# A decoder block for 16 sequences on one core: the second FFN layer as three reduced-precision products

## The chip, the cores and the metric

The program runs on one core of a Trainium2 chip, in one launch. The metric is the device time in microseconds (us). The kernel before was timed three times: 994.58, 998.78 and 999.22 us, median 998.78.

The core's engines work in parallel, each through its own list of instructions in order: PE (TensorE, matrix products into the eight PSUM banks), DVE (VectorE), ACT (ScalarE), POOL (GpSimd), and SP (SyncE), which here only issues DMA transfers. They wait for each other through semaphores.

## The reference, cut to what matters

For each of 16 sequences `x[b]` of 256 tokens by 256 dimensions, with 16 heads of 16 dimensions:

```
x = layernorm(x + self_attention(x))        # q, k: rms norm and rope; causal softmax
x = layernorm(x + cross_attention(x, ctx))  # causal and key mask
x = layernorm(x + ffn(x))

ffn(x) = gelu(rms(x, gamma_l) @ w1_l.T + b1_l) @ w2_l.T + b2_l     # hidden 128, "light"
       + heavy path on the 256 tokens of highest score               # hidden 1024
```

Top-k picks 256 of 256 tokens, and the scores end as factors of one, so the heavy path is applied to every token. The kernel therefore stacks both paths into one FFN with 9 hidden chunks of 128 (`FCH = 9`).

## The kernel before

The weights stay in SBUF. The work of the 16 sequences is a software pipeline written out by hand: `iterations` unrolls steps i = -2 to 19. Step i does the self attention of sequence s = i, most of the cross attention of c = i-1, the end of the cross attention of f = i-2, and the FFN of l = i-3. So an FFN runs in steps 3 to 18, and in steps 3 to 15 all stages are live.

A step has four phases on PE, each a loop over the 16 heads:

- **S1**: `scores(1, s, h)`, the self-attention scores. Each head is three products: the causal mask (`cmaskb`, through the identity), and two blocks of q times k. DVE takes the row maxima from the bank (`mx`, L899). Between heads PE does `hidden(l, j)`, the first FFN layer, at the places of `HIDDEN_AT`.
- **S2**: `scores(2, c, h)`, the same for cross attention. Between heads: transposes of q and k of the next sequence, the value projection, and `ffn_out(l, 0, j)`, the second FFN layer for the first 128 tokens.
- **T1**: `scores_t(1, s, h)`, transposed scores; ACT takes the exponential (`pr`, L746), POOL zeroes the masked part (L1217), and PE multiplies by the values. Between heads `ffn_out(l, 1, j)` for the other 128 tokens.
- **T2**: the same for cross attention, with the projections of later sequences.

Score banks are a ring of three: a head's scores wait until the bank of three heads earlier was read. Between S1 and S2, DVE runs `max_parts(1, s)`: six small operations, each waiting for the one before (L912 to L925), which turn the maxima into three bf16 parts. DVE does the first maximum of S2 only after them.

fp32 products are either plain (`w,g` in `ffn_out`: two PE instructions each) or three products of high and low parts in the type fp32r (`hidden`, and the q, k, v projections of L355 to L361: one PE instruction each). In `ffn_out` one product has 128 hidden rows, 128 tokens and 256 output columns, and there are 9 x 2 x 16 = 288 of them.

q and k are split into three bf16 parts (`nat`), which SP copies by DMA into stacks (`stk`) of 96 rows, six blocks of 16 rows, so that one product gives all cross terms. That is `stack_parts` (L288): 6 transfers of 128 KB for each of q and k.

POOL's list in a step: rope of the next sequence (`rotate`, L241: 12 operations on 128x256 or half of it), x plus bias for the FFN's residual (`x2b`, L1234), low halves of later inputs (`xTlow`, `ctxlow`), a copy, a root, then the masking. ACT's list in a step: copies, the nine gelus (`g`, L758), the table for the exponential, copies, the exponentials.

In the first steps DVE rotates sequence 0 itself, then cuts `wk2` and `wv2` in halves (`halve_cross`) and fills constant rows of the second stacks (`more_rows`), before the first maximum. Scaling and cutting `w1` (`scale_w1`, L1036) follows in step 0, all on DVE.

Of the kernel before, what the change touches and what calls it, by code (L numbers as in the profile page):

```python
# [43 lines left out]
P = 128  # L44
# [19 lines left out]
def build(nc, io):  # L64
# [4 lines left out]
    with ctx:  # L69
# [15 lines left out]
        w1h = sb("w1h", [P, C, FCH * P], f32r); w1l = sb("w1l", [P, C, FCH * P], f32r); w2 = sb("w2", [P, FCH, D])  # L85
# [6 lines left out]
        cmask = sb("cmask", [P, 2, P])  # L92
# [26 lines left out]
        mx2 = sb("mx2", [P, TT, H])  # L119
# [9 lines left out]
        g = sb("g", [P, FCH, T])  # L129
# [7 lines left out]

        w1raw = g[:, :, :].rearrange("p j t -> p (j t)").rearrange("p (c n) -> p c n", c=C)
# [21 lines left out]
        s_const = sem("consts_ready"); s_mask = sem("keybias_step"); s_rows = sem("fixed_rows_ready")  # L160
# [4 lines left out]
        s_qn = sem("qn_ready"); s_rot = sem("pool_rot"); s_rope = sem("rope_ready")  # L165
# [18 lines left out]
        s_h = sem("hidden_ready"); s_g = sem("gelu_ready"); s_out = sem("out_stored"); s_warm = sem("exp_table_loaded")  # L184
# [56 lines left out]
        def rotate(eng, ops, b):  # L241

            for t in range(TT):
# [6 lines left out]
                for s in range(2):  # L250
                    ops.tensor_tensor(qc[:, t, s * D:(s + 1) * D].rearrange("p (h d) -> p h d", d=HD),  # L251
                                    qn[:, t, s * D:(s + 1) * D].rearrange("p (h d) -> p h d", d=HD),
                                    ropeC[:, t, s:s + 1, :].to_broadcast([P, H, HD]), ALU.mult)
                    for half in range(2):
                        last = ops.tensor_tensor(rv[:, s, :, half, :], qv[:, s, :, 1 - half, :],  # L255
                                               ropeS[:, t, s:s + 1, half * h2:(half + 1) * h2]
                                               .to_broadcast([P, H, h2]), ALU.mult)
                last.then_inc(s_rot, 1)
                eng.wait_ge(s_rot, n + 1)

                for s in range(2):
# [3 lines left out]
                                           rot[:, t, s * D:(s + 1) * D].rearrange(pairs, c=C, d=HD), ALU.add)  # L265
                last.then_inc(s_rope, 1)
# [5 lines left out]
        def _(sp):  # L272
# [15 lines left out]
            def stack_parts(a, b, nth, s):  # L288

                terms = (TERMS_Q, TERMS_K)[s]  # L290
                for part, ready in ((0, s_hi[a]), (1, s_mid[a]), (2, s_split[a])):
                    sp.wait_ge(ready, 2 * b + nth + 1)
                    for r in range(len(terms)):
                        if terms[r] == part:
                            load(stk[a][s][r * HD:(r + 1) * HD, :, :], nat[a][s][:, part, :], s_stk[a])

            def stacks(a, b):

                wait(sp, s_st[a], H * b)
                if a == 2:  # L300
                    if first(b):
                        sp.wait_ge(s_rows, 5)
# [42 lines left out]
        def _(pe):  # L345
# [9 lines left out]
            def halves_proj(out, src, t, w):  # L355

                products = [(x, y, c) for x, y in ((src[0], w[0]), (src[0], w[1]), (src[1], w[0])) for c in range(C)]
                for n, (x, y, c) in enumerate(products):
                    last = mm(out, x[:, c, t * P:(t + 1) * P], y[:, c, :], n == 0, n == len(products) - 1)
# [16 lines left out]
            def qk1(b, t):  # L376

                pe.wait_ge(s_xlow, b + 1)
# [5 lines left out]
                halves_proj(bank[QK1_BANK[t]][:, :], xTp, t, wqk1).then_inc(s_qk1, 1)  # L384
# [53 lines left out]
            def hidden(b, j):  # L438

                if j == 0:  # L440
                    if first(b):
                        pe.wait_ge(s_w1, 1)
# [19 lines left out]
            def transpose_qk1(b):  # L462
                pe.wait_ge(s_rope, TT * (b + 1))
# [5 lines left out]

                if live(b - 2):  # L470
# [4 lines left out]
            def scores(a, b, h):  # L475

                if h == 0:
                    if first(b):
                        pe.wait_ge(s_rows, (None, 3, 5)[a])
# [4 lines left out]
                on_pe = a in MASKED_ON_PE  # L484
                if on_pe:
                    blocks = out[:, 0:3 * P].rearrange("p (k t) -> p k t", k=3)
                    mm(blocks[:, 0:3:2, :], idb[:, :], cmaskb[:, :, :], True, False, True)
                mm(out[:, 0:P], q[0:K_MAX, h, 0:P], kk[0:K_MAX, h, 0:P], not on_pe, not on_pe, True)
                mm(out[:, P:3 * P], q[0:K_MAX, h, P:T], kk[0:K_MAX, h, :], not on_pe, True, True)\
# [184 lines left out]
            pe.wait_ge(s_whalf, 2)  # L674
# [5 lines left out]
        def _(act):  # L680
# [53 lines left out]
            def exponential(a, b, h):  # L734
# [9 lines left out]
                else:  # L744
                    act.wait_ge(s_pv[2], NG * (b - 1) + 3 + h // HG)
                nc.scalar.activation(pr[:, h % (2 * HG), :], ring_bank("T", a, b, h)[:, 0:3 * P], ACT.Exp, scale=HD ** -0.5)\  # L746
                    .then_inc(s_exp[a], 1)

            def gelu(b, j):
                act.wait_ge(s_h, FCH * b + j + 1)  # L750
                if j == 0:
                    if first(b):
                        act.wait_ge(s_wffn, 16 * N_FFN)

                        act.wait_ge(s_w1, 1)
# [3 lines left out]
                    .then_inc(s_g, 1)  # L759

            def load_ffn():
                load(w1raw[:, :, 0:LIGHT * P], io["w1h"].rearrange(chunks, p=P), s_wffn)
                load(w1raw[:, :, LIGHT * P:FCH * P], io["w1l"].rearrange(chunks, p=P), s_wffn)
                load(w2[:, 0:LIGHT, :], io["w2h"].rearrange(chunks, p=P), s_wffn)
                load(w2[:, LIGHT, :], io["w2l"], s_wffn)
# [5 lines left out]
            def step(i):  # L771
# [55 lines left out]
                if first(i + 1):  # L827

                    act.wait_ge(s_stk[1], 16 * NSTK[1])
                    load_ffn()  # L830

# [27 lines left out]
        def _(dve):  # L859
# [30 lines left out]
            cm = cmask[:, :, :].rearrange("p k t -> p (k t)")  # L890

# [467 lines left out]
```

## Time and profile before

| | us |
|---|---|
| median of 3 runs | 998.78 |
| lowest, highest | 994.58, 999.22 |
| span of the profiled execution, first to last instruction | 995.1 |
| PE, DVE, ACT, POOL busy | 907.2, 735.8, 496.2, 486.2 |
| one step in the middle | 55.03 |

The profile gives the span of its execution and no separate time for it. The span is 3.7 us under the median, and 0.5 us over the lowest time. Busy time of PE is not PE at its peak, since the products overlap and their ends are modelled; the starts of consecutive instructions are what tell its pace.

### The profile page before, as it was taken

The numbers are of one execution on the slowest core, as the hardware profiler recorded it, in microseconds if no ns is written. First come the engines' busy times: TensorE is split into PE (matmuls) and PEld (weight loads), VectorE is DVE, ScalarE is ACT, GpSimd is POOL, SyncE is SP. The second block draws the span as 40 slices with busy tenths as digits, with TensorE's granted clock in tenths as the row PEclk, the third lists the DMA queues.
The fourth block names the chain that finished last, engine by engine and source line by source line (L and its number), as shares of the span: only waits on it lengthen the run. The fifth ranks groups of instructions, "written<-read, shape, count | busy, mean of one in ns | idle before, by whom it ended". The sixth has DMA issues, their size and how long they took to land.

```text
span 995.1 us, 21915 instructions
## 1 busy us (share of the span) xinstructions
PE 907.2 (91%) x7904; PEld 709.5 (71%) x7904; DVE 735.8 (74%) x1847; ACT 496.2 (50%) x1063; POOL 486.2 (49%) x899
## 2 busy tenths in 40 slices
PE   2467888999999999999999999999999999898896
PEld 2345565787878787787878787877878786777575
DVE  8777678677878878877778788888778787574612
ACT  1131443647465555646474655556464755455243
POOL 2173464545555564645464655646455546143221
PEclk9669899999999999999999999999999999999999
DMA  3909192836657290927566481909365563705000
GB/s 108 180 23 142 24 130 31 118 44 91 83 63 110 37 135 11 132 36 110 63 87 88 55 118 29 129 20 127 46 105 70 77 87 47 115 3 67 22 1 22
DMA packets 79644, 74.24 MB, mean 75 GB/s; under 512 B 8592, under 2 KB 78896, under 8 KB 79536
## 3 DMA queue, kind: packets, MB, share of 16 engines
q1 hardware_dynamic: 75872, 68.90, 49.9%
q10 hardware_dynamic: 3664, 3.94, 1.2%
q8 instruction: 63, 1.03, 0.5%
q14 instruction: 45, 0.37, 0.2%
HBM read 17.49 MB, written 4.20 MB: 22 GB/s over the span
## 4 chain that ended last, share of the span: by engine, by line
PE 56%; DVE 19%; issue 8%; POOL 5%; DMA 4%; SPq 3%; ACT 2%; POOLq 0%; ACTq 0%; DVEq 0%
PE bank L347 53%; DVE mx L899 8%; SPq L274 3%; POOL pr L1217 2%; DMA stk1k<-nat1k 2%; PE bank L372 2%; DVE x L980 2%; PE bank L571 2%; ACT pr L746 2%; DVE qn L1032 1%; DMA stk2q<-nat2q 1%; POOL rstd L1207 1%; DVE nat2q L882 1%; DVE nat2q L884 1%; DVE rest L875 1%
## 5 line engine op out<-in xcount | busy, mean ns | idle before, releaser
L746 ACT ACTIVATE pr<-bank 128x384 f32<-128x384 f32 x512 | 241.0, 501 | 192.4 <-PE bank L347 192.1
L899 DVE TENSOR_REDUCE mx<-bank 128x3 f32<-128x384 f32 x512 | 264.5, 551 | 82.5 <-PE bank L347 80.8
L1217 POOL TENSOR_SCALAR_AFFINE_SELECT pr<-pr 128x256 f32<-128x256 f32 x512 | 225.9, 453 | 183.1 <-ACT pr L746 179.9
L347 PE MATMUL bank<-cmaskb,idb 128*128 128x256 bf16 x512 | 145.2, 284 | 31.5 <-DVE mx L899 15.7
L347 PE MATMUL bank<-w,g 128*128 128x256 f32 x576 | 170.8, 389 | 1.1 <-ACT g L758 1.1
L758 ACT ACTIVATE g<-bank,b 128x256 f32<-128x256 f32 x144 | 68.4, 475 | 90.1 <-PE bank L347 89.8
L1241 POOL TENSOR_TENSOR xTlow<-xT,xThigh 128x512 fp32r<-128x512 f32 x16 | 21.2, 1324 | 161.1 <-ACT xThigh L682 161.1
L347 PEld LDWEIGHTS bank<-w,g 128*128 128x128 f32 x576 | 89.6, 190 | 5.2 <-ACT g L758 1.5
L347 PEld LDWEIGHTS bank<-cmaskb,idb 128*128 128x128 bf16 x512 | 50.3, 98 | 58.9 <-DVE mx L899 32.1
L347 PE MATMUL bank<-stk1k,stk1q 97*128 97x128 bf16 (+1 forms) x512 | 86.6, 258 | 0.0
L347 PE MATMUL bank<-stk1q,stk1k 100*128 100x256 bf16 (+1 forms) x512 | 80.0, 254 | 4.5 <-DMA stk1q<-mT 3.2
L347 PE MATMUL bank<-stk2k,stk2q 97*128 97x128 bf16 (+1 forms) x512 | 82.4, 247 | 0.0
L347 PE MATMUL bank<-stk2q,stk2k 100*128 100x256 bf16 (+1 forms) x512 | 73.0, 252 | 1.8 <-DMA stk2q<-mT 0.9
L347 PEld LDWEIGHTS bank<-stk1q,stk1k 100*128 100x128 bf16 x512 | 42.3, 99 | 38.4 <-ACT pr L746 8.6
L251 POOL TENSOR_TENSOR qc<-qn,ropeC 128x256 f32<-128x256 f32 x60 | 44.2, 737 | 46.6 <-DVE qn L1032 29.6
L347 PE MATMUL bank<-xnh,w1h 128*128 128x256 f32 x288 | 64.7, 306 | 2.3 <-DVE y L952 2.1
L347 PE MATMUL bank<-wo,onT 128*128 128x256 f32 x256 | 63.1, 390 | 1.9 <-ACT onT L682 1.9
L347 PEld LDWEIGHTS bank<-stk2k,stk2q 97*128 97x128 bf16 x512 | 50.6, 99 | 18.9
L255 POOL TENSOR_TENSOR sq<-qn,ropeS 128x128 f32<-128x128 f32 x120 | 60.7, 527 | 0.0
L347 PEld LDWEIGHTS bank<-stk1k,stk1q 97*128 97x128 bf16 x512 | 53.0, 103 | 10.1 <-issue 0.2
L347 PE MATMUL bank<-pr,va 128*32 128x256 f32 (+1 forms) x1024 | 57.1, 342 | 2.4 <-POOL pr L1217 2.3
L347 PE MATMUL bank<-xnl,w1h 128*128 128x256 f32 x288 | 57.6, 281 | 0.0
(157 smaller groups left out, 1829.3 us busy)
## 6 DMA issues: line engine op xcount, KB each, us to landing
stk1q<-nat1q SPq DMA_DIRECT2D x96, 128.0 KB, 4.6
stk1k<-nat1k SPq DMA_DIRECT2D x96, 128.0 KB, 6.5
stk2k<-nat2k SPq DMA_DIRECT2D x96, 128.0 KB, 4.7
stk2q<-nat2q SPq DMA_DIRECT2D x96, 128.0 KB, 6.1
xT<-in_xT SPq DMA_DIRECT2D x16, 256.0 KB, 7.2
ctxT<-in_ctxT SPq DMA_DIRECT2D x16, 256.0 KB, 7.8
x<-in_x SPq DMA_DIRECT2D x16, 256.0 KB, 6.1
out_x<-x SPq DMA_DIRECT2D x16, 256.0 KB, 5.9
```

The costliest lines, as they stand in the source:

```text
L251: ops.tensor_tensor(qc[:, t, s * D:(s + 1) * D].rearrange("p (h d) -> p h d", d=HD), qn[:, t, s * D:(s + 1) * D].rearrange("p (h d) -> p h ...
L255: last = ops.tensor_tensor(rv[:, s, :, half, :], qv[:, s, :, 1 - half, :], ropeS[:, t, s:s + 1, half * h2:(half + 1) * h2] .to_broadcast([ ...
L274: sp.dma_start(dst, src).then_inc(s, 16)
L347: return nc.tensor.matmul(out, lhsT, rhs, start=start, stop=stop, skip_group_check=check)
L372: last = nc.tensor.transpose(bank[k][:, c * T + t * P:c * T + (t + 1) * P], src[:, t, c * P:(c + 1) * P], idf[:, :])
L571: last = nc.tensor.transpose(bank[TOK_BANK[a][t]][:, gr * P:(gr + 1) * P], oT[:, gr, t * P:(t + 1) * P], idf[:, :])
L746: nc.scalar.activation(pr[:, h % (2 * HG), :], ring_bank("T", a, b, h)[:, 0:3 * P], ACT.Exp, scale=HD ** -0.5)\
L758: nc.scalar.activation(g[:, j, :], bank[HIDDEN_BANK[j % 2]][:, 0:T], ACT.Gelu, bias=b1[:, j:j + 1])\
L899: V.tensor_reduce(mx3[:, h, :], scored[:, 0:3 * P].rearrange("p (k t) -> p k t", k=3), AX.X, ALU.max, negate=True).then_inc(s_mx[a], 1)
L980: V.tensor_scalar(xo[a][:, t, :], y[a][:, t, :], mv[a][:, t, 0:1], rstd[a][:, t:t + 1], ALU.subtract, ALU.mult).then_inc(s_x[a], 1)
L1217: G.affine_select(out=slot, in_=slot, compare_op=ALU.is_ge, fill=0.0, base=0, pattern=[[0, 2], [1, P]], channel_multiplier=-1).then_inc(s_ ...
L1241: G.tensor_tensor(xTp[1][:, :, :], xT[:, :, :], xTp[0][:, :, :].bitcast(f32), ALU.subtract)\
```

## The change

- **FFN's second layer.** ACT copies each gelu result `g` to a high part `gh` (fp32r), POOL subtracts to a low part `gl`, and PE does `gh*w2h + gh*w2l + gl*w2h` in place of `g*w2`. `w2` is now loaded in step 0 into `g` and cut in step 1 (ACT `high_w2`, DVE the low half).
- **In place.** The layer norms write over their input (`xo = y`), so `add_residual` now waits for what `layer_norm` waited for. Rope multiplies `qn` in place (`qc = qn`): the sine products come first, with one more wait.
- **Stacks.** Row r of a 16-row part now goes to stack row 6r + n instead of 16n + r. Number and size of the transfers are the same.
- **First steps.** `rotate_first` rotates q of both halves before k, and PE transposes q at once. PE's first projection waits for its parts one by one. The constant rows of the second stacks are filled by POOL (`cross_rows`). `halve_cross` moves on DVE behind the self-attention maxima of step 0. `w1` is scaled and rounded on ACT (`high_w1`), and DVE does only the low half (`low_w1`).
- Code that nothing used is gone (`cmask`, `mx2`), and the SBUF set aside for DMA descriptors is cut to 1024.

```diff
-        xo = [None, sb("x1", [P, TT, D]), sb("x2", [P, TT, D]), sb("x3", [P, TT, D])]
+        xo = y
...
-        qn = sb("qn", [P, TT, 2 * D]); rot = sq; qc = sb("qc", [P, TT, 2 * D]); qr = sb("qr", [P, TT, 2 * D])
+        qn = sb("qn", [P, TT, 2 * D]); rot = sq; qc = qn; qr = sb("qr", [P, TT, 2 * D])
...
-                            load(stk[a][s][r * HD:(r + 1) * HD, :, :], nat[a][s][:, part, :], s_stk[a])
+                            load(stk[a][s][r:NPROD:len(terms), :, :], nat[a][s][:, part, :], s_stk[a])
...
                 if t == 0 and j == 0:
+                    if first(b):
+                        pe.wait_ge(s_w2, 1)
                     pe.wait_ge(s_g, FCH * (b + 1))
-                last = mm(bank[FFN_BANK][:, t * D:(t + 1) * D], g[:, j, t * P:(t + 1) * P], w2[:, j, :],
-                          j == 0, j == FCH - 1)
+                if t == 0:
+                    pe.wait_ge(s_gl, FCH * b + j + 1)
+                for n, (x, w) in enumerate(((gh, w2h), (gh, w2l), (gl, w2h))):
+                    last = mm(bank[FFN_BANK][:, t * D:(t + 1) * D], x[:, j, t * P:(t + 1) * P], w[:, j, :],
+                              j == 0 and n == 0, j == FCH - 1 and n == 2)
...
-                    wait(act, s_o[3], b)
+                    wait(act, s_gl, FCH * b)
...
+            def gelu_high(b, j):
+                act.wait_ge(s_g, FCH * b + j + 1)
+                if j == 0:
+                    wait(act, s_o[3], b)
+                copy(gh[:, j, :], g[:, j, :]).then_inc(s_gh, 1)
...
                     if live(l):
                         gelu(l, j)
+                        if j > 0:
+                            gelu_high(l, j - 1)
+                if live(l):
+                    gelu_high(l, FCH - 1)
...
+                if first(i):
+                    high_w1()
+                if first(i - 1):
+                    high_w2()
...
@@ def add_residual
-                wait(dve, s_x[a], TT * b)
+                if a == 1:
+                    wait(dve, s_x1t, b)
+                    wait(dve, s_x1c, b)
+                elif a == 2:
+                    wait(dve, s_x2b, b)
+                    wait(dve, s_xn, TT * b)
+                else:
+                    wait(dve, s_out, 16 * b)
...
@@ step of DVE
+                if first(i):
+                    halve_cross()
+                    scale_gammas()
...
                 if first(i):
-                    scale_w1()
+                    low_w1()
+                if first(i - 1):
+
+                    dve.wait_ge(s_w2h, 1)
+                    V.tensor_tensor(w2l[:, :, :], w2raw[:, :, :], w2h[:, :, :].bitcast(f32), ALU.subtract).then_inc(s_w2, 1)
...
-                if first(i + 1):
-                    halve_cross()
-                    more_rows()
...
@@ step of POOL, behind x2b
+                    for j in range(FCH):
+                        pool.wait_ge(s_gh, FCH * l + j + 1)
+                        G.tensor_tensor(gl[:, j, :], g[:, j, :], gh[:, j, :].bitcast(f32), ALU.subtract).then_inc(s_gl, 1)
```

The order of the instructions at two places. PE, from the end of S2 into T1 (`w,g` is the plain second layer). Before:

```order
L347 MATMUL bank<-stk2k,stk2q 128x256
L347 MATMUL bank<-w,g 128x256
L347 MATMUL bank<-stk1q,stk1k 128x256
L347 MATMUL bank<-stk1q,stk1k 128x128
L347 MATMUL bank<-w,g 128x256
L347 MATMUL bank<-stk1q,stk1k 128x256
```

And now:

```order
L378 MATMUL bank<-stk2k,stk2q 128x256
L378 MATMUL bank<-w2h,gh 128x256
L378 MATMUL bank<-w2l,gh 128x256
L378 MATMUL bank<-w2h,gl 128x256
L378 MATMUL bank<-stk1q,stk1k 128x256
L378 MATMUL bank<-stk1q,stk1k 128x128
L378 MATMUL bank<-w2h,gh 128x256
```

Each product became three, at the same place between the same heads.

POOL, from the rope of the next sequence to the masking. Before:

```order
L263 TENSOR_TENSOR qr<-qc,sq 128x8x32 x2
L1234 TENSOR_TENSOR x2b<-x,b2sum 128x512
L1241 TENSOR_TENSOR xTlow<-xT,xThigh 128x512
L1247 TENSOR_TENSOR ctxlow<-ctxT,ctxhigh 128x512
L1253 COPY x1c<-x 128x512
```

And now:

```order
L265 TENSOR_TENSOR qr<-qn,sq 128x8x32 x2
L1298 TENSOR_TENSOR x2b<-y,b2sum 128x512
L1303 TENSOR_TENSOR gl<-g,gh 128x256 x9
L1308 TENSOR_TENSOR xTlow<-xT,xThigh 128x512
L1316 TENSOR_TENSOR ctxlow<-ctxT,ctxhigh 128x512
L1322 COPY x1c<-y 128x512
```

Nine subtractions stand where POOL before went straight to `xTlow`.

## Rows read from the trace of the kernel before

**Rows 1.** The page: busy time of the engines.
```profile
PE 907.2 (91%) x7904; PEld 709.5 (71%) x7904; DVE 735.8 (74%) x1847; ACT 496.2 (50%) x1063; POOL 486.2 (49%) x899
```
**Rows 2.** Chain of work that ended last, two middle steps (start us, us, what).
```profile
487.22 11.62 PE bank L347 x84
...
542.25 11.62 PE bank L347 x84
```
**Rows 3.** Timeline of PE (start us, us, what, [idle before <-releaser]): S2, then T1.
```profile
542.25 0.28 PE L347 MATMUL bank<-cmaskb,idb 128*128 128x256 bf16 x1 [0.18 <-DVE mx L899]
...
548.95 0.27 PE L347 MATMUL bank<-cmaskb,idb 128*128 128x256 bf16 x1
...
549.65 0.27 PE L347 MATMUL bank<-cmaskb,idb 128*128 128x256 bf16 x1
...
549.93 0.27 PE L347 MATMUL bank<-cmaskb,idb 128*128 128x256 bf16 x1
...
551.75 0.65 PE L347 MATMUL bank<-w,g 128*128 128x256 f32 x2
552.23 0.33 PE L347 MATMUL bank<-stk1q,stk1k 100*128 100x256 bf16 x2
552.40 0.65 PE L347 MATMUL bank<-w,g 128*128 128x256 f32 x2
```
**Rows 4.** Timeline of PE: before and after twelve fp32r products in T2, six in S1.
```profile
506.09 0.33 PE L347 MATMUL bank<-stk2q,stk2k 100*128 100x256 bf16 x2
...
507.75 0.51 PE L347 MATMUL bank<-stk2q,stk2k 100*128 100x256 bf16 x4
...
538.27 0.27 PE L347 MATMUL bank<-cmaskb,idb 128*128 128x256 bf16 x1
...
539.26 0.28 PE L347 MATMUL bank<-cmaskb,idb 128*128 128x256 bf16 x1
```
**Rows 5.** Timeline of DVE: between S1 and S2, and in S2.
```profile
539.52 0.17 DVE L912 COPY nm<-mx 128x16 f32<-128x16 f32 x1
...
540.58 0.55 DVE L899 TENSOR_REDUCE mx<-bank 128x3 f32<-128x384 f32 x1
...
549.42 0.56 DVE L899 TENSOR_REDUCE mx<-bank 128x3 f32<-128x384 f32 x1 [0.15 <-PE bank L347]
```
**Rows 6.** Timelines of POOL and ACT in the same step.
```profile
534.30 1.26 POOL L1234 TENSOR_TENSOR x2b<-x,b2sum 128x512 f32<-128x512 f32 x1
546.06 1.27 POOL L1241 TENSOR_TENSOR xTlow<-xT,xThigh 128x512 fp32r<-128x512 f32 x1 [10.50 <-ACT xThigh L682]
...
539.46 0.47 ACT L758 ACTIVATE g<-bank,b 128x256 f32<-128x256 f32 x1 [0.81 <-PE bank L347]
```
**Rows 7.** Timelines of DVE and POOL in step 0, when both are at work.
```profile
55.96 0.60 DVE L919 CAST mp<-nm 128x32 bf16<-128x32 f32 x1
...
59.32 1.63 DVE L884 TENSOR_TENSOR nat1q<-rest,nat1q 128x512 bf16<-128x512 f32 x1
...
55.08 1.45 POOL L263 TENSOR_TENSOR qr<-qc,sq 128x256 f32<-128x256 f32 x2
58.96 1.44 POOL L1241 TENSOR_TENSOR xTlow<-xT,xThigh 128x512 fp32r<-128x512 f32 x1 [2.43 <-ACT xThigh L682]
```
**Rows 8.** Timelines of the first steps: DVE, then ACT.
```profile
44.37 1.76 DVE L1153 MEMSET stk2q<- 1x2048 f32 x1 [0.38 <-issue]
46.17 0.56 DVE L899 TENSOR_REDUCE mx<-bank 128x3 f32<-128x384 f32 x1
...
67.55 2.64 DVE L1050 TENSOR_TENSOR w1l<-g,w1h 128x2304 fp32r<-128x2304 f32 x1
...
61.65 0.49 ACT L746 ACTIVATE pr<-bank 128x384 f32<-128x384 f32 x1 [2.25 <-PE bank L347]
```
**Rows 9.** Waits: PE for transfers of the first stack of k (total us, times, longest).
```profile
PE bank L347 <- DMA stk1k<-nat1k: 11.7, 4, 5.8
```
**Rows 10.** Timeline of PE near the end: the second layer with nothing between.
```profile
962.73 8.04 PE L347 MATMUL bank<-w,g 128*128 128x256 f32 x36 [0.56 <-ACT g L758]
```

More of the change, by code:

```diff
@@ L257, in rotate @@
                                                .to_broadcast([P, H, h2]), ALU.mult)
+                last.then_inc(s_turn, 1)
+                eng.wait_ge(s_turn, n + 1)
+                for s in range(2):
+                    last = ops.tensor_tensor(qc[:, t, s * D:(s + 1) * D].rearrange("p (h d) -> p h d", d=HD),
+                                    qn[:, t, s * D:(s + 1) * D].rearrange("p (h d) -> p h d", d=HD),
+                                    ropeC[:, t, s:s + 1, :].to_broadcast([P, H, HD]), ALU.mult)
                 last.then_inc(s_rot, 1)
@@ L353, in tok_proj, with halves_proj @@
                 return last
-            def halves_proj(out, src, t, w):
-                products = [(x, y, c) for x, y in ((src[0], w[0]), (src[0], w[1]), (src[1], w[0])) for c in range(C)]
+            def halves_proj(out, src, t, w, as_they_come=False):
+                products = [(x, y, c) for x, y in ((src[0], w[0]), (src[1], w[0]), (src[0], w[1])) for c in range(C)]
                 for n, (x, y, c) in enumerate(products):
+                    if as_they_come and n == 0:
+                        pe.wait_ge(s_xhigh, 1)
+                        pe.wait_ge(s_whalf, 1)
+                    if as_they_come and n == C:
+                        pe.wait_ge(s_xlow, 1)
+                    if as_they_come and n == 2 * C:
+                        pe.wait_ge(s_whalf, 2)
                     last = mm(out, x[:, c, t * P:(t + 1) * P], y[:, c, :], n == 0, n == len(products) - 1)
@@ L376, in qk1 @@
             def qk1(b, t):
-                pe.wait_ge(s_xlow, b + 1)
+                at_start = first(b) and t == 0
+                if not at_start:
+                    pe.wait_ge(s_xlow, b + 1)
                 wait(pe, s_qn, TT * b)
@@ L462, in transpose_qk1 @@
             def transpose_qk1(b):
-                pe.wait_ge(s_rope, TT * (b + 1))
+                pe.wait_ge(s_rope, 1 if first(b) else TT * (b + 1))
                 if live(b - 3):
@@ L477, in scores @@
                 if h == 0:
-                    if first(b):
-                        pe.wait_ge(s_rows, (None, 3, 5)[a])
+                    if first(b) and a == 1:
+                        pe.wait_ge(s_rows, 3)
+                    elif first(b):
+                        pe.wait_ge(s_crows, 2)
                     pe.wait_ge(s_stk[a], 16 * NSTK[a] * (b + 1))
@@ L483, in scores @@
                 q, kk = stk[a]
[L484 to L489, printed above, removed]
+                blocks = out[:, 0:3 * P].rearrange("p (k t) -> p k t", k=3)
+                mm(blocks[:, 0:3:2, :], idb[:, :], cmaskb[:, :, :], True, False, True)
+                mm(out[:, 0:P], q[0:K_MAX, h, 0:P], kk[0:K_MAX, h, 0:P], False, False, True)
+                mm(out[:, P:3 * P], q[0:K_MAX, h, P:T], kk[0:K_MAX, h, :], False, True, True)\
                     .then_inc(s_s[a], 1)
@@ L745, in exponential @@
                     act.wait_ge(s_pv[2], NG * (b - 1) + 3 + h // HG)
+                if a == 1 and first(b) and h == HG:
+                    act.wait_ge(s_chalf, 4)
                 nc.scalar.activation(pr[:, h % (2 * HG), :], ring_bank("T", a, b, h)[:, 0:3 * P], ACT.Exp, scale=HD ** -0.5)\
@@ L830, in step, with high_w1 @@
                     load_ffn()
+                if first(i):
+                    load_w2()
+            def high_w1():
+                act.wait_ge(s_gam, 1)
+                for c in range(C):
+                    for which, lo, hi in ((0, 0, LIGHT * P), (1, LIGHT * P, FCH * P)):
+                        nc.scalar.activation(w1h[:, c, lo:hi], w1raw[:, c, lo:hi], ACT.Copy, scale=gam[:, which, c:c + 1])\
+                            .then_inc(s_halved, 1)
             def squares(b, t):
@@ L1106, in step @@
                     statistics_cross()
+                if first(i):
+                    halve_cross()
+                    scale_gammas()
                 if live(f):
@@ L1242, in step @@
                         .then_inc(s_xlow, 1)
+                if first(i + 2):
+                    cross_rows()
                 if live(s):
@@ L1276, in step, with cross_rows @@
                         roots[h]()
+            ones_pair = float(np.array([0x3F803F80], np.uint32).view(np.float32)[0])
+            def cross_rows():
+                pool.wait_ge(s_xlow, 1)
+                G.memset(stk[2][1][ROW_BIAS:K_ALL, :, :].bitcast(f32), ones_pair).then_inc(s_crows, 1)
+                pool.wait_ge(s_crows, 1)
+                G.memset(stk[2][0][ROW_BIAS:ROW_BIAS + 1, :, :].bitcast(f32), ones_pair).then_inc(s_crows, 1)
+                pool.wait_ge(s_crows, 2)
             for m in (idf, idb):
@@ L1280, in _ @@
             G.memset(minus_half[:, :], -0.5)
[L1281 to L1282 removed]
+            G.memset(cmaskb[:, :, :], 0.0).then_inc(s_pool, 1)
             for v in (*va1, va2):
@@ L1288, in _ @@
                                 pattern=[[-1, P]], channel_multiplier=1)
-            for diag, n in ((cmask[:, 1, :], 1), (cmaskb[:, :, :], 2)):
-                G.affine_select(out=diag, in_=diag, compare_op=ALU.is_ge, fill=BIG, base=0,
-                                pattern=[[0, 2], [-1, P]][2 - n:], channel_multiplier=1)
+            G.affine_select(out=cmaskb[:, :, :], in_=cmaskb[:, :, :], compare_op=ALU.is_ge, fill=BIG, base=0,
+                            pattern=[[0, 2], [-1, P]], channel_multiplier=1)
             for v in (*va1, va2):
```

121 lines of the change are left out of this document (62 added, 59 removed).

## The prediction, on record before the change was timed

> **What bounds the kernel now.** I read the busy times first: PE has work for 91% of the span, the next engine (DVE) for 74% [rows 1]. That alone doesn't say what a saved PE microsecond is worth, so I went to the chain of work that ended last, in two middle steps. The same piece of 84 PE instructions starts at 487.22 and at 542.25: one step lasts 55.03 us, and S2 and T1 hang on PE without a break [rows 2]. What stands ahead of that piece decides as much. At 542.25 PE had waited 0.18 us for DVE's maximum [rows 3]: it had caught up with DVE, which was late because it ran `max_parts(1, s)` from 539.52 until the first maximum of S2 at 540.58, 1.06 us for six dependent small operations [rows 5]. Later in S2 DVE waits 0.15 us per head for PE [rows 5]. So in S2 and T1 a shorter PE counts, and at the border S1/S2 a longer DVE counts, each in full. Seen from the whole, 13 steps (3 to 15) are full; the first three and the last three are ruled by latencies.
>
> **PE's second layer.** In S2 a head with a plain product takes 549.65 - 548.95 = 0.70 us, one without 549.93 - 549.65 = 0.28 [rows 3]: the product costs 0.42. In S1 a head with six fp32r products takes 539.26 - 538.27 = 0.99 us [rows 4]; less 0.28 that is 0.71, or 0.118 each. Three cost 0.355, so 0.07 less. In T1 the plain product costs 552.23 - 551.75 = 0.48, a pair of scores 0.17 [rows 3]. In T2, 507.75 - 506.09 = 1.66 holds a pair and twelve fp32r products [rows 4]; less 0.17 and nine at 0.118 that leaves 0.43 for the first three. There 0.05 is saved. Per step 9 x 0.07 + 9 x 0.05 = 1.1 us, over 13 steps **-14 us**. The bounds are nothing, if three products break PE's flow between heads as no row shows, and -20, if T1 saves 0.12 as three at 0.118 would.
>
> The Trainium skill (FP8 and Floating Point Precision, TensorE Precision Notes) says that true FP32 takes four passes through the array. With three single passes in their place a quarter would go, some 0.11 us per product, and by that the sum would be 11 us better. The rows give about half, because each fp32r product takes 0.118 us where a quarter of the plain one is 0.105; I go by the rows.
>
> **ACT's nine copies** to `gh` cost less than a gelu of the same size each, 0.47 us [rows 6]. ACT is half idle [rows 1] and waits for PE's banks; the last gelu ends at 539.93, then come two copies more, over 5 us before POOL gets the `xThigh` of this step, at 546.06 [rows 6]. Nothing. The first product waits for all gelus as before.
>
> **POOL's nine subtractions.** `xTlow` has twice their size and takes 1.27 us [rows 6], so 0.66 each, 6 us together. POOL is free from 535.56 to 546.06, waiting 10.50 us for ACT [rows 6]; its time is paid for by that. They can't end early: `gh` of j is behind the gelu of j+1, the last two follow the gelu of 539.46, so the row of subtractions is unbroken from 535.6 to about 541.7. PE wants the first at 541, the last at 550: no wait. But `max_parts(1, s)` runs from 539.52 to 540.6, in the midst of it. In step 0 DVE and POOL met: a cast of `max_parts` took 0.60 us beside rope's additions on POOL, where the six take 1.06 together; a subtraction of two SBUF tensors requested at 59.32 took 1.63 us and ended 0.5 us after POOL's `xTlow` (58.96 + 1.44 = 60.40) [rows 7]. DVE waited for POOL's whole instruction. Here the first two operations wait 0.1 us for the running subtraction, and then the first cast, perhaps the subtraction behind it, and the second cast each meet a new one: 0.35 to 0.6 us each. That gives 0.8 us if the subtraction passes, 1.5 if not; I take **1.3 us**, nearer the second for the 1.63 of rows 7. PE at 542.25 has no slack, and everything behind it is chained: 13 x 1.3 = **+17 us**. Bounds: 0 (no meeting) and 2.5 (five full waits in place of the two or three).
>
> **The other edits in the steady steps.** In place: `add_residual` now waits for `x2b`, `x1T` and `xn` of the sequence before, all over 5 us old there (x2b ends at 535.56, the cross residual is at 541), and for a store issued half a step before. Rope has two more waits of POOL on itself, 0.1 us, with 10.50 us of cover [rows 6]. The stacks' new rows change no count; PE waits for the first stack of k four times in the run, 11.7 us together, the longest 5.8 at the start [rows 9], so in steady steps nothing comes of it. Zero for all three. Gone code: zero, it never ran.
>
> **The first steps.** The first maximum stands at 46.17, right behind a fill of 1.76 us and its twin [rows 8]: DVE, not the scores, is late there. Without the two fills (3.5 us) and the four operations of `halve_cross` (some 2 us), and with q rotated first, DVE starts at 39 to 40: 6.5 us sooner. Not all of it lives. ACT now does `high_w1` (four activations, 2.5 us by its gelu's pace) ahead of `xThigh` and `ctxhigh`, and waits for the gammas, which stand on DVE behind `halve_cross`; the first exponential (61.65 [rows 8]) comes at 58, POOL's masks at 60. That is 2 us kept, and 2 more since DVE no longer scales and rounds `w1` beside those masks, and does one pass over it, like the 2.64 of rows 8, where it did three. In step 1 the pass for `w2l`, as long, stands beside the masks and takes 1 us back; I allow 0.5 gain for the rest. **-3.5 us** (0 to -7).
>
> **The end.** In steps 17 and 18 the second layer stands alone: 8.04 us for 36 instructions [rows 10], now 54 x 0.118 = 6.4. That is 2 x 1.6. Step 16 gives 0.8 more: **-4 us**. `gh` and `gl` of the last chunk (0.4 + 0.7 us) are hidden by the eight triples ahead (2.8 us). If not, 1 us per step is lost, so -2 at the least.
>
> **Sum.** -14 + 17 - 3.5 - 4 = -4.5, and 1 us less for the ring waits that a late DVE swallows on PE (0.18 of [rows 3], in part of the steps): **-5.5 us**. Against the profiled span of 995.1 that is 989.6; the span lies 3.7 under the median of the three runs, so on the median, 998.78, it is **993.3 us**. About 0.5% (5 us) is what a measurement of this kernel can tell from no change; the forecast stands on that edge.
>
> **Rivals.**
> - *DVE and POOL don't meet to harm.* For it: the maxima themselves read PSUM, and ran at 0.55 beside rope. Against: [rows 7]. Then -14 - 7.5, about 977 to 981.
> - *The border S1/S2 costs over 2.1 us* (slower). One mechanism: each of the small dependent operations, the two-input ones as well, comes just after POOL has begun a new subtraction and waits for all of it; slowed by DVE's turns the row of subtractions lasts beyond 542.5. At 2.4 us: 13 x (2.4 - 1.1) - 7.5 = +9.5, 1008; it ends slower than the median from 1.7 us on and slower by 0.5% from 2.1.
> - *Three products cost what the plain one did* (the change doesn't do its work): for it only that no row has three alone between heads of bf16. 993.3 + 14 + 3 = 1010.
> - *The stacks land faster.* PE's 11.7 us of waiting [rows 9] are in the first steps and in the last; were transfers a third shorter, 3 to 4 us would go: 990. Beside it: the Trainium skill (SBUF — State Buffer, Door 1: The DMA port swizzle) says that bandwidth depends on how many of the SBUF's 16 ports the partitions reach, and that 16 adjacent ones reach four. Rows six apart reach more; no row here shows spread rows.
>
> **How the numbers follow.** Forecast, border cost 0.8 to 1.5: 0.50, of which 0.27 below 993.8 and 0.23 within 5 us. No meeting: 0.17, faster. Border over 1.7: 0.12, of which 0.04 within and 0.08 slower. No saving on PE: 0.06, slower. Faster stacks: 0.15, 0.10 faster and 0.05 within. Faster 0.54, same 0.32, slower 0.14. The forecast's own range is 987 to 999. The range of 8 in 10 reaches from 978 (most of the first rival) to 1005 (the milder half of the second).
>
> **What would show it.** In a middle step: from `cmaskb` to `cmaskb` of a head in S2 with a triple 0.63 to 0.64 in place of 0.70, a head of T1 0.60 in place of 0.65. `max_parts(1, s)` 2.3 us in place of 1.06, its casts over 0.5 us each, beside `gl` on POOL; PE waiting for `mx` at the third and fourth head of S2. The step's length 55.2. First maximum near 39.5, first exponential near 58; 6.4 us for the last 54 products. I am wrong on the cause if `max_parts` stays at 1.1 us, and on the sum if the step isn't within 54.7 to 55.6.

## The result and the profile after

The change makes the kernel slower, where the forecast was a gain of half a per cent.

| | before | after |
|---|---|---|
| median of 4 runs each, us | 996.86 | 1012.3 |
| lowest, highest, us | 994.58, 999.22 | 1011.36, 1013.88 |
| ratio after to before, 95% interval | | 1.0155 (1.013 to 1.018) |
| span of the profiled execution, us | 995.1 | 1009.3 |

1012.3 us lies outside the range of 978 to 1005 and on the side that had a chance of 0.14. (With a fourth run the median of before is 996.86; the three that the forecast went by gave 998.78.) The page of the kernel after, busy time (against [rows 1]), the granted clock in 40 slices, and SP's queue:

```profile
PE 902.4 (89%) x8192; PEld 730.5 (72%) x8192; DVE 753.7 (75%) x1845; ACT 542.3 (54%) x1212; POOL 594.2 (59%) x1043
...
PEclk8767999999999999999999999999999999999988
...
q1 hardware_dynamic: 75872, 68.90, 24.4%
```

PE is busy for 4.8 us less and the program still takes 14.2 us more, so PE waits. (At the full clock it would be some 20 us less: the page of e1 below, with the same products, has 887.1.) The last row holds a surprise of its own, a queue that needs a quarter of the DMA engines' time where before it needed 49.9%. The chain of waits shows how long a step is (start, us, what; against [rows 2]):

```profile
492.46 10.78 PE bank L378 x97
...
548.41 12.35 PE bank L378 x97
...
605.97 12.32 PE bank L378 x97
```

One step takes 605.97 - 548.41 = 57.56 us, another 548.41 - 492.46 = 55.95, where all had 55.03. And the same 97 instructions on PE take 10.78 us in one step and 12.35 in another. There are 13 such pieces, three short ones (at 263.69, 492.46 and 720.98) and ten long ones. So two things have to be found: 0.9 us in every step, and 1.57 us in ten of 13.

The border between S1 and S2. Timeline of DVE after (start, us, what; against [rows 5]):

```profile
543.70 0.61 DVE L980 COPY nm<-mx 128x16 f32<-128x16 f32 x1
544.22 0.78 DVE L981 TENSOR_TENSOR nm<-mx 128x16 f32<-128x16 f32 x1
545.03 0.66 DVE L985 CAST mp<-nm 128x32 bf16<-128x32 f32 x1
545.73 0.66 DVE L987 TENSOR_TENSOR nr<-nm,mp 128x32 f32<-128x32 f32 x1
546.42 0.18 DVE L989 CAST mp<-nr 128x32 bf16<-128x32 f32 x1
546.63 0.19 DVE L991 TENSOR_TENSOR mp<-nr,mp 128x32 bf16<-128x32 f32 x1
546.74 0.55 DVE L975 TENSOR_REDUCE mx<-bank 128x3 f32<-128x384 f32 x1
```

and of POOL in the same stretch (against [rows 6]):

```profile
538.87 1.26 POOL L1298 TENSOR_TENSOR x2b<-y,b2sum 128x512 f32<-128x512 f32 x1
540.09 6.25 POOL L1303 TENSOR_TENSOR gl<-g,gh 128x256 fp32r<-128x256 f32 x9
```

`max_parts(1, s)` lasts from 543.70 to 546.74, 3.04 us in place of 1.06. POOL's row of nine subtractions runs from 540.09 to 546.34. The four operations that fall into it take 0.6 to 0.8 us, the two behind it 0.18 and 0.19. Two of the four that were held are plain two-input operations.

What PE makes of it, in the same step (against [rows 3]):

```profile
547.35 0.28 PE L378 MATMUL bank<-cmaskb,idb 128*128 128x256 bf16 x1 [1.68 <-DVE mx L975]
...
548.41 0.38 PE L378 MATMUL bank<-cmaskb,idb 128*128 128x256 bf16 x1 [0.39 <-DVE mx L975]
...
552.34 0.28 PE L378 MATMUL bank<-cmaskb,idb 128*128 128x256 bf16 x1
...
552.98 0.28 PE L378 MATMUL bank<-cmaskb,idb 128*128 128x256 bf16 x1
...
558.07 0.34 PE L378 MATMUL bank<-stk1q,stk1k 100*128 100x256 bf16 x2
...
558.66 0.34 PE L378 MATMUL bank<-stk1q,stk1k 100*128 100x256 bf16 x2
```

PE waits 1.68 and 0.39 us, at the fourth and fifth head of S2. Later in S2 a head with three products takes 552.98 - 552.34 = 0.64 us (before 0.70), a head of T1 558.66 - 558.07 = 0.59 (before 0.65): the triples are as cheap as forecast. Just behind the wait, though, PE is slow. Busy time and granted clock of the 3.6 us from the start of the piece of 97, a long one and a short one:

```profile
548.41:552.01 3.60, 3.60 (x19) 3.39 (x20) 3.13 (x10) 0.00 (x0) 0.00 (x0) 0.53 0.03 7
492.46:496.06 3.60, 3.60 (x33) 3.42 (x33) 3.56 (x12) 1.06 (x3) 0.00 (x0) 1.00 0.02 7
```

In the first, PE gets 0.53 of its clock, that is nearly all the time the lower of its two levels, 1.2 GHz in place of 2.4, and issues 19 products where it issues 33 in the other. The ten long pieces show 0.53 to 0.65 there, the three short ones 1.00; in the four steps of before that I read it is 1.00.

The start and the end, which were forecast apart: DVE's first maximum, ACT's first exponential, and the second layer alone near the end (against [rows 8] and [rows 10]):

```profile
38.46 0.55 DVE L975 TENSOR_REDUCE mx<-bank 128x3 f32<-128x384 f32 x1
...
56.81 1.60 ACT L794 ACTIVATE pr<-bank 128x384 f32<-128x384 f32 x4
...
978.57 6.63 PE bank L378 x54
```

### The profile page after: what moved, and what is told of

The parts are those of the page before. It is cut to its first block, busy times and chain, and to the rows that moved or that the text cites. A ratio compares the mean times of both kernels' runs of the same rounds, so it can differ in the third digit from the quotient of the medians.

```text
span 1009.3 us, 22799 instructions
## 1 busy us (share of the span) xinstructions
PE 902.4 (89%) x8192; PEld 730.5 (72%) x8192; DVE 753.7 (75%) x1845; ACT 542.3 (54%) x1212; POOL 594.2 (59%) x1043
## 3 DMA queue, kind: packets, MB, share of 16 engines
q8 instruction: 65, 1.06, 0.4%
## 4 chain that ended last, share of the span: by engine, by line
PE 58%; DVE 22%; issue 7%; POOL 5%; ACT 3%; SPq 0%; DMA 0%; DVEq 0%; POOLq 0%; ACTq 0%
PE bank L378 54%; DVE mx L975 8%; POOL pr L1281 3%; ACT pr L794 2%; DVE y L1044 2%; PE bank L612 2%; PE bank L410 2%; DVE qn L1096 2%; DVE nat2q L963 1%; DVE y L1025 1%; POOL rstd L1271 1%; DVE nm L981 1%; DVE nr L987 1%; DVE mp L985 1%; DVE nat2q L961 1%
## 5 line engine op out<-in xcount | busy, mean ns | idle before, releaser
L378 PE MATMUL bank<-cmaskb,idb 128*128 128x256 bf16 x512 | 147.6, 288 | 38.9 <-DVE mx L975 37.6
L1303 POOL TENSOR_TENSOR gl<-g,gh 128x256 fp32r<-128x256 f32 x144 | 101.5, 734 | 27.3 <-ACT gh L727 26.8
L378 PE MATMUL bank<-w2h,gh 128*128 128x256 f32 x288 | 102.8, 357 | 1.1 <-ACT g L806 1.1
L378 PE MATMUL bank<-stk2k,stk2q 97*128 97x128 bf16 (+1 forms) x512 | 85.1, 253 | 0.0
L378 PE MATMUL bank<-w2l,gh 128*128 128x256 f32 x288 | 81.8, 284 | 0.0
L378 PE MATMUL bank<-w2h,gl 128*128 128x256 f32 x288 | 81.5, 283 | 0.0
L378 PE MATMUL bank<-xnh,w1l 128*128 128x256 f32 x288 | 58.3, 284 | 0.0
```

The costliest lines, as they stand in the source:

```text
L378: return nc.tensor.matmul(out, lhsT, rhs, start=start, stop=stop, skip_group_check=check)
L1303: G.tensor_tensor(gl[:, j, :], g[:, j, :], gh[:, j, :].bitcast(f32), ALU.subtract).then_inc(s_gl, 1)
```

## Experiments

In all of them theory A is that the nine subtractions on POOL hold DVE's six small operations, and that the wait this gives PE brings the low clock. The ratios are to runs of the kernel before on the same chip, with 95% intervals.

### The subtractions in two parts (e1_gl_pause)

```diff
                     for j in range(FCH):
+                        if j == 4 and live(s):
+                            pool.wait_ge(s_mp[1], s + 1)
                         pool.wait_ge(s_gh, FCH * l + j + 1)
```

> After, with one more wait on POOL: the fifth to ninth of the nine subtractions of gl start only when max_parts(1, s) is through. Theory A (the subtractions hold the six small operations of DVE between S1 and S2 for 2.0 us per step, and TensorE, which waits for them, then gets a low clock, 1.6 us in 10 of 13 steps): max_parts back at 1.1 to 1.5 us, granted clock 1.00 at the start of S2, 1012.3 - 13 x 2.0 - 10 x 1.6 = 970, at most 5 more if the last subtraction before the pause still overlaps. Rival B (the three products on TensorE, with their denser work, bring the low clock, the border only 2.0 us): 986. Rival C (ACT's copies, the in-place waits or the new rope order cost the time): within 3 of 1012.

Measured: 972.18 us, 0.9755 (0.973 to 0.9779), the fastest kernel of this study; all parts of the change are in it. DVE and POOL at the border:

```profile
530.61 0.17 DVE L980 COPY nm<-mx 128x16 f32<-128x16 f32 x1
530.70 0.17 DVE L981 TENSOR_TENSOR nm<-mx 128x16 f32<-128x16 f32 x1
...
531.67 0.55 DVE L975 TENSOR_REDUCE mx<-bank 128x3 f32<-128x384 f32 x1
...
527.01 2.79 POOL L1305 TENSOR_TENSOR gl<-g,gh 128x256 fp32r<-128x256 f32 x4
531.83 3.48 POOL L1305 TENSOR_TENSOR gl<-g,gh 128x256 fp32r<-128x256 f32 x5 [2.03 <-DVE mp L991]
```

`max_parts` is back at 531.67 - 530.61 = 1.06 us, all 13 pieces of 97 take 10.77 or 10.78, and a step is 54.0 to 54.1 us long. One wait moves the kernel by 40 us: rivals B and C are out.

### No subtractions at all (e2_no_gl)

```diff
-                        G.tensor_tensor(gl[:, j, :], g[:, j, :], gh[:, j, :].bitcast(f32), ALU.subtract).then_inc(s_gl, 1)
...
-                for n, (x, w) in enumerate(((gh, w2h), (gh, w2l), (gl, w2h))):
+                for n, (x, w) in enumerate(((gh, w2h), (gh, w2l), (gh, w2h))):
```

> After without the nine subtractions of gl (the low half of the gelu's result is left out); TensorE's third product takes gh in its place, so TensorE and ACT do as much as in after. Theory A: max_parts 1.06 us, the step 54.0 to 54.2 us, granted clock 1.00 at the start of S2, 968 to 971. Rival B (the low clock comes from the three products): 984 to 988. Rival C (ACT's copies, in-place waits, rope order): above 1005.

Measured: 972.81 us, 0.9764 (0.9739 to 0.9789). The same as with the pause, so POOL's 6.3 us per step cost nothing when they don't meet `max_parts`. The forecast had that part right.

### Everything but the new second layer (e3_plain_second_layer)

```diff
-                for n, (x, w) in enumerate(((gh, w2h), (gh, w2l), (gl, w2h))):
-                    last = mm(bank[FFN_BANK][:, t * D:(t + 1) * D], x[:, j, t * P:(t + 1) * P], w[:, j, :],
+                last = mm(bank[FFN_BANK][:, t * D:(t + 1) * D], g[:, j, t * P:(t + 1) * P], w2h[:, j, :],
```

> After with the plain second layer of before (one fp32 product, no gh, no gl, w2 not cut); the in-place edits, rope order, stack rows and first steps stay. Theory A: the other edits cost nothing in the steady steps and gain some 8 us in the first, so the step is 55.0 us and the whole 988 to 990. Rival C (the in-place waits or the rope order cost something in each step): the step above 55.3 us, the whole above 993. Against the run without gl the difference is what three products gain on TensorE: 13 steps x 0.9 + 5 at the end = 17 us.

Measured: 984.26 us, 0.9873 (0.9842 to 0.9903), 3.7 us under the lower end of what was expected. The step is 54.85 us, 0.18 shorter than before, which is 2.3 us of it over 13 steps. Nearly all of the 0.18 stands in one operation of DVE in S1, beside POOL's rope. Timelines of DVE and POOL before, then in this run:

```profile
529.35 0.79 DVE L882 CAST nat2q<-rest 128x512 bf16<-128x512 f32 x1
...
529.12 0.73 POOL L251 TENSOR_TENSOR qc<-qn,ropeC 128x256 f32<-128x256 f32 x1
529.81 1.51 POOL L255 TENSOR_TENSOR sq<-qn,ropeS 128x128 f32<-128x128 f32 x2
```

```profile
464.79 0.62 DVE L948 CAST nat2q<-rest 128x512 bf16<-128x512 f32 x1
...
464.68 2.33 POOL L251 TENSOR_TENSOR sq<-qn,ropeS 128x128 f32<-128x128 f32 x4
```

A cast of this shape takes 0.43 alone. Before, it came upon a rope product of 128x256 (0.73 us) and had to let it end at 529.81; in the new order a sine product of half the size runs there, and it gets through 0.17 us sooner. So the rope's order, priced at nothing, gave 0.17 us per step by the same meeting that costs so much at the border. That is read from the rows: no run has the rope's order alone, and up to 0.03 of the 0.18 can be the stacks' rows (the step of e5 below is 55.00).

The other expectation was missed: from here to e2 it is 11.5 us, not 17. The step gives 0.85 (54.86 to 54.01), and behind the last of the 13 pieces 3.5 us go, the 0.85 of that step among them. But e2 reaches its first piece at 208.37 us and e3 at 203.24, and that eats 5 us of the gain in the profiled executions.

### A later border without POOL (e4_late_border, e8_border_1p4)

The kernel before, with DVE reading a weight behind `max_parts(1, s)`, three times in e4 (shown) and twice in e8:

```diff
                     max_parts(1, s)
+                    if live(l):
+                        for n in range(3):
+                            V.tensor_reduce(pad[:, n:n + 1], wo1[:, :, :].rearrange("p c n -> p (c n)"), AX.X, ALU.max)
```

> Before with three more reductions of a weight (128x512 from SBUF, 0.69 us each, 2.07 together, their results unused) on DVE behind max_parts(1, s), in steps 3 to 18 where s is alive (13 of them). Nothing else is changed and POOL is idle there. Theory A (each us at this border counts in full, and a wait of TensorE of this length there brings the low clock): 13 x 2.1 = 27 for the border, and the low clock in some or most of the steps, 1.6 each: 1024 to 1045, clock below 0.7 behind the border where it is low. Rival B (low clock only with the three products): clock 1.00 there, 1024. Rival D (the border has slack in before): below 1015.

> Before with two reductions of 0.69 us behind max_parts(1, s) in place of three: a border longer by 1.38 us, close to the 1.3 us that the prediction took. Theory A3 (the low clock comes only where TensorE waits longer than this): 996 + 13 x 1.55 = 1016, clock 1.00 behind the border in all steps. Theory A4 (it comes here too): the same with 1.56 us in some ten steps, 1032.

Measured: e4 1036.13 us, 1.0408 (1.0373 to 1.0443); e8 1014.39 us, 1.0188 (1.0162 to 1.0214). PE at the border, and the pieces of 84 of which the second follows it, in e4:

```profile
500.51 0.28 PE L347 MATMUL bank<-cmaskb,idb 128*128 128x256 bf16 x1 [1.39 <-DVE mx L899]
...
501.57 0.28 PE L347 MATMUL bank<-cmaskb,idb 128*128 128x256 bf16 x1 [0.39 <-DVE mx L899]
```

```profile
444.79 11.62 PE bank L347 x84
...
501.57 13.17 PE bank L347 x84
```

and PE in e8:

```profile
551.69 0.28 PE L347 MATMUL bank<-cmaskb,idb 128*128 128x256 bf16 x1 [0.80 <-DVE mx L899]
...
552.76 0.28 PE L347 MATMUL bank<-cmaskb,idb 128*128 128x256 bf16 x1 [0.39 <-DVE mx L899]
```

Back to back a reduction takes 0.60 us, so the border is longer by 1.8 and 1.2 us; the steps are 501.57 - 444.79 = 56.78 us, 1.75 more than before, and 56.20, 1.17 more. Each us at this border counts in full. With waits of 1.39 + 0.39 us PE gets the low clock in nine of 13 steps, with 0.80 + 0.39 in none. The other four steps of e4 have the same two waits and a granted clock of 1.00 (the piece at 444.79 is one), so the length of the wait alone doesn't decide it, and what does stays open. Neither kernel has the new products: the low clock belongs to the wait.

### Work for PE in the wait (e9_filled_wait)

```diff
+            def fill(n):
+                for _ in range(n):
+                    mm(bank[FFN_BANK][:, 3 * P:4 * P], idb[:, :], idb[:, :], True, True, True)
...
+                    if live(s):
+                        add(FFN0_AT[0], fill, 24)
```

> After with 24 small products more on TensorE (128x128 by 128x128 bf16, results unused), put where TensorE waits 1.68 us behind the border, in the steps where all is alive; about 1.3 us of work by the pace of the scores. max_parts stays held by the subtractions. Theory A5 (it is the wait that brings the low clock, so work in it keeps it high): clock 1.00 at the start of S2 in all steps, the step 55.95 in all, 1012.3 - 10 x 1.56 = 997, at most 3 more. Rival F (the low clock comes from something else at this border): 1012 to 1016.

Measured: 998.26 us, 1.0002 (0.9976 to 1.0027). The added products write to the bank in which the second layer's sum for the first 128 tokens is under way, so this kernel serves for its time alone.

```profile
542.37 1.51 PE L378 MATMUL bank<-idb 128*128 128x128 bf16 x24
544.22 0.28 PE L378 MATMUL bank<-cmaskb,idb 128*128 128x256 bf16 x1 [0.34 <-DVE mx L981]
```

DVE is held as in after, but all 13 pieces of 97 take 10.77 to 10.80 us, and a step is 56.1 us. 24 useless products save 14 us. That closes the second half of the theory.

### What holds what (e6_copies_beside, e10_gl_in_halves, e7_gl_all_behind)

```diff
+                        if j == 0 and live(s):
+                            pool.wait_ge(s_mx[1], H * (s + 1))
...
-                        G.tensor_tensor(gl[:, j, :], g[:, j, :], gh[:, j, :].bitcast(f32), ALU.subtract).then_inc(s_gl, 1)
+                        G.tensor_copy(gl[:, j, :], g[:, j, :]).then_inc(s_gl, 1)
```

> After, but POOL's nine subtractions of gl are copies of g (one input, about 0.3 us each, so the low half is left out) and start right behind the last maximum of S1, at the same time as max_parts(1, s). Theory A1 (DVE's operation waits for the end of any POOL instruction on SBUF): each of the six waits 0.15 to 0.3 us, max_parts 2.0 to 2.6 us, 13 x 1.2 = 16 us over the run with the pause, 985 to 1000 with the low clock in part of the steps. Theory A2 (only an instruction with two inputs holds DVE): max_parts 1.1 us, 968 to 973.

```diff
-                        G.tensor_tensor(gl[:, j, :], g[:, j, :], gh[:, j, :].bitcast(f32), ALU.subtract).then_inc(s_gl, 1)
+                        for t in range(TT):
+                            last = G.tensor_tensor(gl[:, j, t * P:(t + 1) * P], g[:, j, t * P:(t + 1) * P],
+                                                   gh[:, j, t * P:(t + 1) * P].bitcast(f32), ALU.subtract)
+                        last.then_inc(s_gl, 1)
```

> After with each of the nine subtractions of gl cut in two of 128x128 (18 of about 0.4 us). Theory A6 (a small operation of DVE waits for the end of the POOL instruction that runs, not for the row of them): the waits shrink with the length, max_parts 1.06 + 4 or 5 x 0.3 = 2.2 to 2.5 us in place of 3.04, TensorE's wait 1.1 us or less at the border, so no low clock or only in a few steps, 988 to 1002. Rival G (DVE is held as long as POOL has the next one ready, whatever its length): max_parts 3.0 or more, 1010 to 1016.

```diff
+                        if j == 0 and live(s):
+                            pool.wait_ge(s_mp[1], s + 1)
```

> After, with all nine subtractions of gl behind max_parts(1, s) in place of the last five. Theory A: as the run with the pause at the fifth, 970 to 974, max_parts 1.06 us. Rival E (four more subtractions beside S2 hold DVE's residual and its other two-input work there, and xTlow, ctxlow and the copy come later): 0.5 to 1.0 us per step, 978 to 985.

Measured: e6 983.3 us, 0.9869 (0.9847 to 0.989); e10 986.27 us, 0.9902 (0.9874 to 0.993); e7 977.92 us, 0.981 (0.9786 to 0.9835). DVE and POOL in e6:

```profile
534.18 0.32 DVE L985 CAST mp<-nm 128x32 bf16<-128x32 f32 x1
534.53 0.32 DVE L987 TENSOR_TENSOR nr<-nm,mp 128x32 f32<-128x32 f32 x1
...
533.71 3.18 POOL L1305 CAST gl<-g 128x256 fp32r<-128x256 f32 x9 [3.59 <-DVE mx L975]
```

and in e10:

```profile
480.62 0.39 DVE L987 TENSOR_TENSOR nr<-nm,mp 128x32 f32<-128x32 f32 x1
...
475.92 7.51 POOL L1304 TENSOR_TENSOR gl<-g,gh 128x128 fp32r<-128x128 f32 x18
```

A POOL instruction takes 3.18 / 9 = 0.35 us in e6, 7.51 / 18 = 0.42 in e10 and 6.25 / 9 = 0.69 in after; a held operation of DVE takes 0.32, 0.39 and 0.66 (`nr` and the casts), just under the length of POOL's own each time, and the next one starts 0.35 us later in e6 and 0.70 in after. So the rows read as if DVE gets its turn once at each boundary between two POOL instructions, and its next operation waits for the next one. One input on POOL's side is enough (A2 is out). `max_parts` takes 1.78 us in e6 and 2.25 in e10, and both have the full clock in all steps. Both totals came out 1.7 us below the lower end that was expected, and `max_parts` in e6 0.2 us below its own (2.0).

e7 has `max_parts` at 1.06 us, as theory A said, but not theory A's total (970 to 974): it ends at the lower edge of its rival's range (978 to 985), by another way. DVE's residual is not held in S2: a residual with one input in PSUM and one in SBUF takes its usual time beside the subtractions. It is PE that waits, for the first of them:

```profile
477.57 0.68 DVE L1025 TENSOR_TENSOR y<-bank,x1c 128x512 f32<-128x512 f32 x1
```

```profile
478.14 0.35 PE L378 MATMUL bank<-w2h,gh 128*128 128x256 f32 x1 [0.48 <-POOL gl L1305]
```

With a step of 54.5 us that is 0.5 us more than with the pause in the middle.

### The rows of the stacks (e5_spread_rows, e11_packed_rows)

e5 is the kernel before with the new rows; e11 is e3 with the old rows.

```diff
-                            load(stk[a][s][r * HD:(r + 1) * HD, :, :], nat[a][s][:, part, :], s_stk[a])
+                            load(stk[a][s][r:len(terms) * HD:len(terms), :, :], nat[a][s][:, part, :], s_stk[a])
```

> Before with one edit, the new stack rows: row r of a 16-row part goes to stack row 6r + n in place of 16n + r. Theory R (the transfers land in 2.4 us in place of 4.6 to 6.5 because of the rows, and PE's 11.7 us of waiting for the first stacks is what can be saved): share of q1 about a quarter in place of a half, the whole 3 to 6 us shorter, 990 to 993, the step still 55.0. Rival (the shorter landings come from the other first steps, not from the rows): landings as before, 995 to 997.

> After with the plain second layer, and the stack rows as before too (part n in rows 16n to 16n + 15), so that only the first steps, the in-place edits and the rope order are left of the change. If the rows are worth the 4.7 us that they gained on before, whatever stands beside them: 984.3 + 4.7 = 989, the step 54.85, q1 at about half the share. If the first steps gain only with fast stacks: 993 to 995, the stacks of k waited for in the first steps and again behind the last full step. If the rows are worth nothing beside the new first steps: 984 to 985.

Measured: e5 991.99 us, 0.9952 (0.9932 to 0.9971); e11 996.34 us, 0.9994 (0.9982 to 1.0006). Queue and landing in e5, then in e11:

```profile
q1 hardware_dynamic: 75872, 68.90, 24.9%
...
stk1k<-nat1k SPq DMA_DIRECT2D x96, 128.0 KB, 2.4
```

```profile
q1 hardware_dynamic: 75872, 68.90, 49.8%
...
stk1k<-nat1k SPq DMA_DIRECT2D x96, 128.0 KB, 6.4
```

The rows alone bring the landing from 6.5 to 2.4 us and take 4.7 us off the run; 3.0 us of it lie between the last two pieces of 84 (53.27 us apart in e5, 56.27 before), where PE before waited for a stack of k. By the Trainium skill (SBUF — State Buffer, Door 1: The DMA port swizzle) the bandwidth of a transfer depends on how many ports its partitions reach; these runs agree, with 24.9% of the engines' time against 49.8 for the same bytes. And the rest of e3 is worth nothing without them (e11, 0.9994), but 7.7 us with them (991.99 - 984.26). Some 2 us in both are the rope's, since the step of e11 is 54.85 too; so by these medians the new first steps alone give some 5 us with the new rows and cost 1 or 2 without them. In e11 the time that DVE gains is spent waiting for the first stacks, as the chain of waits shows:

```profile
79.31 8.48 DMA stk1k<-nat1k
...
97.69 7.77 DMA stk2q<-nat2q
```

## Why the prediction was wrong

By its steps, per full step where not said otherwise:

| step of the prediction | forecast, us | measured, us |
|---|---|---|
| PE's second layer | -1.1 | -0.89 |
| border S1/S2 ("POOL's nine subtractions") | +1.3 | +1.98 |
| PE's clock behind the border | no term | +1.57 in 10 of 13 steps |
| rope, in-place waits | 0 | -0.17 |
| before the first border, whole run | -3.5 | -7.9 |
| from the last but one of the 13 pieces on, whole run | -4 | -7.0 |

With 13 borders: 13 x 1.98 = +25.7, 10 x 1.57 = +15.7, 12 x (-0.89 - 0.17) = -12.7 for the distances between them, -7.9 and -7.0. That makes +13.8, where the spans differ by 14.2. The -0.89 is what a step of 55.95 us leaves when the other two terms are taken out of it (e2 against e3 gives -0.85). The -7.9 is the first piece's start, 206.16 for 212.09, less the 1.98 in it; the -7.0 is what the last interval and the tail show (55.05 for 56.27 us, and 119.6 for 121.4) beyond the terms above.

**The step that failed** is "POOL's nine subtractions", and in it two things. The place, the meeting and the length of the row (6.25 us for a forecast 6) were right. The size was not: I let the first two operations off with 0.1 us and gave the two-input ones a half chance to pass, where [rows 7] held the answer in the 1.63 us of a subtraction of two SBUF tensors. Each of the four operations that fell into the row waited: 0.44, 0.61, 0.48 and 0.47 us over their times alone. The first two, forecast at 0.1, are thus half of the sum; the second cast, which I had meeting a subtraction too, ran behind the row. The sum, 2.0, was within the bounds of 0 to 2.5 that the text gave, and the rival "over 2.1" was its neighbour. It cost 0.7 x 13 = 9 us. The other was missing altogether: the sum took a wait of PE as worth its own length, and 15.7 us of low clock had no term. Borders longer by 1.17 us (e8) and 1.19 (e10) left the clock alone, those longer by 1.75 (e4) and 1.98 did not; the 1.3 us which I took lie between, next to the first two, and no run has them. Together the two make an error of 25 us, of which the better start, the better end and the rope hid some 9. Without the second the run would have been at about 997, within the range, but by these gains and not because the border was right. By the prediction's own sign, a step outside 54.7 to 55.6, the sum was wrong: the steps are 55.95 and 57.5 us. And the 1 us taken off for ring waits wasn't there: the 1.19 us that DVE was held up in e8 cost 1.17 per step.

The Trainium skill (SBUF — State Buffer, Who interferes with whom) has the rule that I should have put on DVE's side: a copy or cast in a two-port mode, or an operation with both inputs in SBUF, contends with GpSimd for a shared pair of ports, and whoever issues first has it for its whole instruction. These runs agree: four copies, casts and two-input operations held in after, the reductions from PSUM (0.55 us) and the residual with one PSUM input (0.68) not.

**PE's second layer** came out as argued. PE reaches its last scores of T1 1.1 us earlier (16.02 us behind the start of the piece in e1, 17.13 before), the forecast figure. Then it waits for POOL's mask, and the next product starts 550.34 - 549.36 = 0.98 us behind those scores, where before it was 0.77, so 0.9 remains:

```profile
550.34 0.86 PE L378 MATMUL bank<-pr,va1b 128*32 128x256 f32 x16 [0.33 <-POOL pr L1281]
```

By the four passes of the Trainium skill (FP8 and Floating Point Precision, TensorE Precision Notes) a product would have gained an estimated 0.11 us; the trace gives half, 0.70 - 0.64 = 0.06.

**ACT's copies** cost nothing (e2, e1), as said. **The end**: 54 products in 6.63 us (6.4 forecast), with the last of `gh` and `gl` hidden. Of the -7.0, 3.0 are by e5 the stacks', and 1.1 belong to the thirteenth step, which the forecast counted elsewhere; that leaves 2.9 for the forecast's 4.

**The first steps** began as forecast, the first maximum at 38.5 (39.5) and the first exponential at 56.8 (58), but the gain then grew in place of shrinking, since the stacks landed sooner. The rival on the stacks was given as another way to go; it was true together with all the rest, and e11 shows that it carries the gain of the first steps. Their size is the least certain of the table: after and e1 run the same instructions up to the first border, and reach it 5 us apart in their profiled executions, with different granted clocks on the way. After is the fast one; by e1's 209.01 us the row would read -3.1, about the forecast.

## What to carry to other kernels

Before work is moved to POOL, list DVE's small dependent operations on SBUF in the same stretch: here each took about as long as one POOL instruction (0.69 us) in place of its own 0.2. The price went with one semaphore wait that parts the row of POOL's work around them, and from 1.98 us to 1.19 with POOL instructions cut in two. And a wait of PE is not worth its length alone: read the granted clock just behind it.

## What the runs showed of the hardware that was not expected

- Waits of PE of 1.39 and 0.39 us, parted by a few products, were enough for the low level of its clock over most of the next 3.6 us, 1.57 us of time, in nine of 13 steps (e4); 0.80 and 0.39 us never were, nor 0.88 and 0.39 (e10). The steps that escape have the same waits as the others. In after (1.68 and 0.39 us) they are the second, sixth and tenth, in e4 the first, second, fifth and tenth.
- PE's useless products in such a wait are worth more here than they cost (998.26 against 1012.3).
- With rows six apart the other transfers of SP land sooner too: `xT` in 3.1 us in e5 and 3.0 in after, 7.2 before, though their own form is unchanged.
